# The product of probabilities and values in an attention stage: two plain fp32 products in place of six of rounded halves and rests

## What is computed

```python
q = (hidden_states @ Wq).reshape(B, Sq, H, D)
k = (encoder_hidden_states @ Wk).reshape(B, Skv, H, D)
v = (encoder_hidden_states @ Wv).reshape(B, Skv, H, D)
q = rmsnorm(q, gq)
k = rmsnorm(k, gk)
scores = jnp.einsum('bqhd,bkhd->bhqk', q, k) * scale
attn = jax.nn.softmax(scores, axis=-1)
out = jnp.einsum('bhqk,bkhd->bqhd', attn, v)
return out.reshape(B, Sq, H * D) @ Wo
```

## Time and profile before

| | |
|---|---|
| timed executions, us | 1266.77, 1267.17, 1268.74 |
| span of the profiled execution, us | 1266.5 |
| TensorE busy in the span | 866.9 us, 68% |
| VectorE busy | 813.6 us, 64% |
| ScalarE busy | 498.3 us, 39% |
| GpSimd busy | 330.0 us, 26% |
| mean granted TensorE clock | 0.813 |
| attention of the first batch, from its first scores to its residual | 697.8 to 758.4 us |

### The profile page before, as it was taken

One profiled execution on the slowest core, in us unless ns is written; L12 is line 12 of the kernel. 1 busy time (PEld: TensorE's weight loads), 2 busy tenths in 40 slices (PEclk: granted clock), 3 DMA queues, 4 the chain that ended last, 5 costly groups with the idle time before them and its releaser, 6 DMA issues.

```text
span 1266.5 us, 16161 instructions
## 1 busy us (share of the span) xinstructions
PE 866.9 (68%) x4324; PEld 657.8 (52%) x4324; DVE 813.6 (64%) x2012; ACT 498.3 (39%) x1242; POOL 330.0 (26%) x344
## 2 busy tenths in 40 slices
PE   2114863587348842884588997969789797879756
PEld 1003631565136621762375785749667595658635
DVE  4896789569875888468430776348653676438653
ACT  3331422233122421252147445545365453555332
POOL 4744462326221643122020002120023001130023
PEclk9555975799558955896689997989899897989857
DMA  3150000010001000112300000010000100000000
GB/s 128 66 230 13 0 1 1 1 46 0 0 0 46 0 0 0 67 67 104 121 30 12 2 5 1 1 35 1 5 0 0 35 1 5 0 21 1 1 1 9
DMA packets 12190, 33.48 MB, mean 26 GB/s; under 512 B 2121, under 2 KB 5585, under 8 KB 10321
## 3 DMA queue, kind: packets, MB, share of 16 engines
q1 hardware_dynamic: 12112, 32.70, 7.3%
HBM read 30.59 MB, written 2.10 MB: 26 GB/s over the span
## 4 chain that ended last, share of the span: by engine, by line
issue 51%; DVE 18%; PE 14%; POOL 11%; ACT 3%; DMA 1%; DVEq 1%; POOLq 1%; SPq 0%; ACTq 0%
PE bk L944 13%; DVE pool L1497 2%; POOL acl L591 2%; POOL pool L559 2%; DVE pool L1503 2%; POOL ac L597 2%; DVE t L1523 1%; DVE pool L1489 1%; DMA pool<-in_wo 1%; POOL lnr L531 1%; POOL fside L619 1%; POOL q7bd L619 1%; DVE v L1636 1%; POOL ac L572 1%; POOL v L581 1%
## 5 line engine op out<-in xcount | busy, mean ns | idle before, releaser
L559 POOL TENSOR_TENSOR pool<-pool 128x512 f32<-128x512 f32 x64 | 94.1, 1470 | 124.4 <-DVE pool L1503 124.0
L531 POOL TENSOR_TENSOR lnr<-lnv,mhalf 128x2 f32<-128x2 f32 x20 | 16.9, 845 | 419.0 <-DVE lnv L1402 418.7
L1523 DVE SCALAR_TENSOR_TENSOR t<-th,bk 128x256 f32<-128x256 f32 (+1 forms) x120 | 50.1, 417 | 107.6 <-ACT th L760 106.5
L944 PE MATMUL bk<-hT,first 128*128 128x256 f32 (+1 forms) x448 | 113.2, 400 | 0.0
L751 ACT ACTIVATE ssm_da<-m,nega 128x255 f32<-128x255 f32 x128 | 57.7, 499 | 118.5 <-DVE pool L1497 104.9
L944 PE MATMUL bk<-early,first 128*128 128x256 f32 x384 | 96.5, 389 | 0.0
L944 PEld LDWEIGHTS bk<-hT,first 128*128 128x128 f32 (+1 forms) x448 | 87.9, 200 | 15.7 <-issue 1.0
L944 PE MATMUL bk<-bc,sel 96*128 96x512 bf16 (+1 forms) x128 | 52.8, 419 | 58.6 <-DVE pool L1503 45.6
L1497 DVE TENSOR_TENSOR_SCAN pool<-ssm_da,pool 128x512 f32<-128x512 f32 x64 | 90.2, 1409 | 0.4
L944 PE MATMUL bk<-first,ac 128*128 128x256 f32 (+1 forms) x224 | 65.2, 416 | 28.9 <-POOL ac L572 28.9
L760 ACT ACTIVATE th<-bk 128x256 f32<-128x256 f32 x88 | 33.9, 385 | 127.1 <-PE bk L944 126.8
(11 more groups left out here) (353 smaller groups left out, 2381.7 us busy)
## 6 DMA issues: line engine op xcount, KB each, us to landing
out<-xo SPq DMA_DIRECT2D x8, 256.0 KB, 2.6
pool<-in_wo SPq DMA_DIRECT2D x4, 512.0 KB, 4.6
first<-in_wq SPq DMA_DIRECT2D x1, 2048.0 KB, 9.0
first<-in_wd SPq DMA_DIRECT2D x1, 1792.0 KB, 16.6
first<-in_wg SPq DMA_DIRECT2D x1, 1760.0 KB, 8.6
first<-in_wu SPq DMA_DIRECT2D x1, 1760.0 KB, 12.3
xin<-in_x SPq DMA_DIRECT2D x4, 256.0 KB, 3.0
pool<-in_q3u SPq DMA_DIRECT2D x1, 1024.0 KB, 5.1
```

The source lines that it names most:

```text
L531: g.tensor_tensor(lnr, lnv, mhalf[:, 0:2], ALU.pow).then_inc(*sig(f"{k}.pool", "lnr"))
L559: g.tensor_tensor(sy, sy, ssm_u[:, n % 3, :].rearrange("p (e t) -> p e t", e=2), ALU.add).then_inc(*sig("s0.pool", "y", n))
L944: return t_.matmul(dst, lhsT, rhs, start=start, stop=stop)
L1523: v.scalar_tensor_tensor(out=quarter(t1, c)[0:m, :], in0=quarter(th, c)[0:m, :], scalar=1.0, in1=bank[0:m, 0:S], op0=ALU.add, op1=ALU.mult ...
```

## The change

The turned probabilities go to SBUF by one ScalarE copy of 128x512 in plain fp32 (`pT4`, two buffers, which the sixth and later layers use too), and P.V is two plain fp32 products, one for each block of 128 keys, straight from `cx`. The subtractions on VectorE, the split of the context and their semaphores go. TensorE's wait for the buffer of the turned probabilities moves from VectorE's "pl" to ScalarE's "pT" of the same head.

```diff
-        pTh4 = [[hTh[:, 0, :], hTh[:, 1, :]], [ach[0][:, :], ach[1][:, :]]]
-        pTl4 = [[hTl[:, 0, :], hTl[:, 1, :]], [acl[0][:, :], acl[1][:, :]]]
-        cxh4, cxl4 = [t[2][:, :].rearrange("p (k c) -> p k c", k=2) for t in (ach, acl)]
...
     def probsT(b, k, j, bank):                      # ScalarE
                 if j >= 2:
                     act.wait_ge(*at(b, f"{k}.pe", "o", j - 2))
-                if k == "s6":
-                    s.activation(pT4[0], halves(bank), ACT.Copy).then_inc(*sig("s6.act", "pT", j))
-                else:
-                    for kc in range(2):
-                        s.activation(pTh4[j % 2][kc], bank[:, kc * S:kc * S + S], ACT.Copy).then_inc(*sig("sa.act", "pT", j, kc))
+                s.activation(pT4[j % 2], halves(bank), ACT.Copy).then_inc(*sig(f"{k}.act", "pT", j))
...
     def attention(b):                               # ScalarE
-                act.wait_ge(dma_sem("loadC"), b * 16 + 16)
-                s.activation(cxh4, cx[:, :, :], ACT.Copy).then_inc(*sig("sa.act", "cx"))
...
     def probsT(b, k, j):                            # TensorE
-                    pe.wait_ge(*at(b, "sa.dve", "pl", j - 2, 1))
+                    pe.wait_ge(*at(b, "sa.act", "pT", j - 2))
...
     def attention(b):                               # TensorE
-                        pe.wait_ge(*at(b, "sa.dve", "pl", h0, 1))
-                        parts = [(cxh4, pTh4), (cxl4, pTh4), (cxh4, pTl4)]
+                        pe.wait_ge(*at(b, "sa.act", "pT", h0))
                         for kc in range(2):
-                            for q, (c4, p4) in enumerate(parts):
-                                m = mm(OPB[i % 2][:, 0:S], c4[:, kc, :], p4[h0 % 2][kc],
-                                       start=kc == 0 and q == 0, stop=kc == 1 and q == 2)
+                            m = mm(OPB[i % 2][:, 0:S], cx[:, kc, :], pT4[h0 % 2][:, kc, :], start=kc == 0, stop=kc == 1)
...
     def attention(b):                               # VectorE
-                dve.wait_ge(*at(b, "sa.act", "cx"))
-                v.tensor_tensor(cxl4, cx[:, :, :], cxh4.bitcast(F32), ALU.subtract).then_inc(*sig(K, "cl"))
...
-                    if 0 <= i - 2 < NH:
-
-                        m = i - 2
-                        dve.wait_ge(*at(b, "sa.act", "pT", m, 1))
-                        for kc in range(2):
-                            v.tensor_tensor(pTl4[m % 2][kc], PTB[m % 2][:, kc * S:kc * S + S], pTh4[m % 2][kc].bitcast(F32),
-                                            ALU.subtract).then_inc(*sig(K, "pl", m, kc))
```

## The result

The changed kernel takes 1270.55 us (median of ten executions, 1269.38 to 1271.63), the kernel before 1267.32 in ten executions beside it (1266.61 to 1269.03). The ratio is 1.0024, 95% interval 1.0015 to 1.0034: slower by 3.2 us. Forecast were 7.8 us more. The sign was right, the forecast was more than twice what came, and 1270.55 lies just inside the lower edge of the stated range (1270.5).

The account below looks back on a forecast made before the run. TensorE's work was taken as the bound in mid-attention, 3.44 us per head. Head costs of +8.5 us over four batches less 0.7 at the jumps gave +7.8: 1267.17 to 1275.0 us, range 1270.5 to 1279.5 for 8 in 10.

Parts of the forecast that it names:

- P.V, the term that decides: Context product on TensorE, per head: two plain fp32 products cost 0.86 us in place of 0.71 for six, +0.15.
- The rule of four passes: Skill page on TensorE: true fp32 takes four passes; P.V from 0.64 to 0.85 us, +0.21 per head; not used.
- Which heads pay: Per attention stage: head 0 pays 0.08 us, heads 1 to 14 2.10, head 15 -0.06; sum 2.12, four batches +8.5.
- VectorE's subtractions worth nothing: VectorE, 2 x 0.41 us less per head: nothing in mid-pipeline; taken as 0, at most 0.1 us per batch.
- head 15: Last head of each attention: +0.15 us for P.V, minus a 0.21 wait for VectorE's last subtraction, gives -0.06.
- the 1.05 us ahead of the exponentials: ScalarE's wait once per head, read as a wait for TensorE.
- The stand at the jump: VectorE between batches: only the first subtraction behind the jump goes, 2 x 0.35 = 0.7 us gain; 3.45 us stand unchanged.
- Rival 2: VectorE's stand after two jumps depends on list length or code place: up to 6.9 us goes, 1268.1; chance 0.07.
- The clock behind the attentions: TensorE's half-clock stretches may fall otherwise as stages shift 2 to 8 us; shifts go both ways, nothing in the sum.
- bad draws: Half-clock stretch 3.4 us longer where TensorE bounds costs 1.7 us; two to four give 1278.4 to 1281.8; chance 0.10.
- the 0.7 us between span and median: Profiled span of the kernel before, 1266.5 us, lies 0.7 below its median; difference added to the median.

Follow-up runs that it names:

- experiment 4: Changed kernel with VectorE's two subtractions per head put back dead, TensorE again waiting for them: 1270.06 us, ratio 1.0019 to the kernel before.
- experiment 7: Kernel before with only the two hi.hi products of P.V, copies and subtractions kept, output incomplete: 1240.09 us, ratio 0.9780.
- experiment 1: Changed kernel with the context split (ScalarE's copy, VectorE's subtraction) put back dead at each attention's start: 1269.90 us, ratio 1.0017 to the kernel before.
- Experiment 3: Kernel before with one dead VectorE reduction (128x1500) once ahead of the phase B loop: 1266.60 us against 1267.90 beside it, ratio 0.9990.
- split late: Kernel before with VectorE's context-split subtraction moved behind the first two scalings of k: 1264.61 us, ratio 0.9977.

## Why the prediction was wrong in size

**P.V, the term that decides: right.** 0.86 us per head for two fp32 products in place of 0.71 was measured as 0.86, and the period rose from 3.44 to 3.60. Experiments 4 and 7 show by themselves that TensorE's work is the period. The rule of four passes (the Trainium skill, "FP8 and Floating Point Precision", section TensorE Precision Notes), taken with one pass for each rounded product, gave an estimate of 0.21 per head for the extra; the trace says 0.16, and the forecast's choice to go by the rows was the better one.

**Which heads pay: right.** 2.12 us per attention were forecast, 1.99 to 2.03 measured. The wait of the last P.V went, as said. In four batches the term was 0.5 us too high, most of it in head 15: its P.V before took 0.81 us to the next `down` (754.61 to 755.42), not 0.71, so that stretch fell by 0.15 and not by 0.06.

**VectorE's subtractions worth nothing: right** (0.08 us per attention in experiment 4). One row was misread beside this: the 1.05 us ahead of the exponentials were ended by VectorE's negative maximum, not by TensorE. Nothing in the sum hangs on it.

**The stand at the jump: this step failed.** The sum counted the instruction behind the jump (0.35 us, seen in experiment 1) and put any change of the 3.45 us ahead of it at nothing. The stand fell by 1.0 and 1.3 us. Rival 2 had named this, with 6.9 us at most and a chance of 0.07; it came true for 2.2 us. The argument against it was that ScalarE stands about as long behind its own jump with quite another list. That another engine also stands says nothing about what the length of this stand hangs on. The shorter list was known from the change, and the prediction counted too little of it: VectorE's body loses 50 entries (508 to 458), three for each of 16 heads and two for the split, not "some two dozen". The experiments tie the stand to this list; why it falls at 508 and not gradually stays open.

**The clock behind the attentions: this step failed too.** I wrote that shifts go both ways and then gave a price only to bad draws, above the forecast; in the sum the term was nothing. In the profiled pair it was -2.4 us: the half clock behind each of the first three attentions lasted 10.2 us instead of 13.6. Experiment 3 shows such shorter stretches in a kernel without the change. A forecast from rows with the long stretches should have given a price to the good draws too.

How much of the 3.2 us between the medians is such a draw is not settled, because the draw also changes from execution to execution of one kernel. Beside the experiments the kernel before ran 59 times: 15 executions with a mean granted clock of 0.815 or more have a median of 1266.6 us, the other 44 one of 1268.3. And the first four layers, the same code in all eleven profiled kernels, ended between 694.5 and 697.9 us. The ten executions of the two kernels do not overlap (1266.61 to 1269.03 against 1269.38 to 1271.63), so that the changed one is slower is not the draw of an execution. The profiled one of the kernel before was itself somewhat slow: in those 59, the time is 1.66 to 1.82 us above the span, which puts it, as an estimate, at 1268.2 us, about 0.9 above its median. The prediction had taken the 0.7 us between span and median as what lies outside the span.

In the profiled pair the forecast of 7.8 and the measured 2.5 differ by 5.3 us: 2.2 are the stand, 2.4 the clock behind the attentions, 0.5 the smaller term of the heads, 0.2 the stretch ahead. The medians differ by 0.7 more than the pair. Of these 0.7, about 0.3 lie outside the span (2.0 us in the changed kernel's executions, 1.7 in those of the kernel before); the rest is within what executions differ by.

## What to carry to other kernels

Fewer instructions are no gain where the bound engine's time per operand type grows: price the new form from a row of the same shape, and add up start times to see whether the engine has any gap. When a loop body gets shorter or longer, read the engines' stand at the jump as a term of its own with a range. And where stages alternate between a busy TensorE and an idle one, moving them by a few microseconds can change how much work falls on half clock: repeat a surprising gain or loss with a dead delay before believing it, and read more than one execution.

## What the runs showed that I had not expected

- A dead 1.72 us reduction made the kernel before no slower (0.9990, 0.9979 to 1.0001) and the changed one slower (1.0044 against 1.0024).
- VectorE's stand at a jump back is 3.6 to 3.9 us with 508 entries in the body and 2.6 to 2.95 with 458 to 506.
- The same kernel's executions differ by up to 8 us (split late, 1261.73 to 1269.98), and their mean granted clocks with them (0.822 to 0.811).
- An attention stage that fills at half clock for longer takes 1.2 us more (58.8 against 57.6, 60.8 against 59.6).
- The split late, a change of order of one instruction, gave the only kernel with the whole result that is faster than before: 1264.61 us, 0.9977 (0.9959 to 0.9995). In its profile most of the gain lies in stretches that the edit does not touch, where the clock fell otherwise, so it may not last in another setting.
